# Odd blocks of x read in 128-byte pieces and turned by VectorE; outer-product tables in parts of four heads; a new prologue

## The reference

```python
def _L0_cond_ref(u, length, log_dt, C, log_A_real, A_imag, D):
    u_m = u * mask[:, None, :]
    kernel = _get_kernel(log_dt, C, log_A_real, A_imag, Lq)   # [H, L]: 2 Re sum_n Cs exp(dtA l)
    y = irfft(rfft(u_m, 2L) * rfft(kernel, 2L))[..., :L]
    return (y + u_m * D[:, None]) * mask[:, None, :]
def _L0_ffn_ref(x, route_w, A, Bw):                # E=8 experts, rank R=16
    logits = einsum('bsd,ed->bse', x, route_w)
    route_weight = one_hot(argmax(logits)) * max(logits)
    h = einsum('bsd,erd->bser', x, A)
    return einsum('bser,eor->bso', route_weight[..., None] * h, Bw)
x = x + _L0_ffn_ref(_L0_cond_ref(x, ...), ...)
```

## Time and profile before

| | us |
|---|---|
| median of 3 runs | 623.53 |
| profiled execution | 623.93 |
| its span | 622.1 |
| TensorE busy | 591.5 (95%) |
| VectorE busy | 542.5 (87%) |
| ScalarE busy | 379.3 (61%) |
| GpSimd busy | 372.9 (60%) |

### The profile page before, as it was taken

The page is one execution under the profiler, slowest core; times in us unless marked ns, Lnnn a source line. Parts: engine busy times, 40 slices in busy tenths (PEclk is TensorE's granted clock), DMA queues, the critical chain, the costliest instruction groups (busy, mean ns, idle before and its releaser), DMA issues.

```text
span 622.1 us, 13886 instructions
## 1 busy us (share of the span) xinstructions
PE 591.5 (95%) x3681; PEld 530.9 (85%) x3681; DVE 542.5 (87%) x1436; ACT 379.3 (61%) x1164; POOL 372.9 (60%) x474
## 2 busy tenths in 40 slices
PE   3379999999999999999999999999999999999995
PEld 2268998999899889988998998899899989988984
DVE  7778889988988898899889888988998898889874
ACT  3676656766676666567666766665676667666520
POOL 4465566557656755675576567556755765676520
PEclk9989999999999999999999999999999999999998
DMA  6023534453454345435534543454345345434521
GB/s 137 17 56 108 152 110 128 147 150 96 142 149 132 113 139 153 112 126 146 152 96 139 151 133 110 141 152 114 125 146 152 98 136 151 139 105 140 154 78 67
DMA packets 37074, 77.68 MB, mean 125 GB/s; under 512 B 11836, under 2 KB 20350, under 8 KB 36998
## 3 DMA queue, kind: packets, MB, share of 16 engines
q1 hardware_dynamic: 27846, 43.76, 29.5%
q10 hardware_dynamic: 9152, 33.03, 13.0%
HBM read 43.16 MB, written 33.62 MB: 123 GB/s over the span
## 4 chain that ended last, share of the span: by engine, by line
PE 92%; DVE 4%; issue 2%; POOL 1%; ACT 0%; DMA 0%; POOLq 0%
PE psYo L987 19%; PE psZ L1009 19%; PE psO L987 15%; PE psYe L987 12%; PE psS L987 11%; PE psO L1036 5%; PE psXe L1000 4%; PE psXo L1000 4%; PE psZ L1078 1%; PE psS L1047 1%; DMA logs<-in_L_cond_log_dt_dram 0%; DVE ex L693 0%; POOL Grev L436 0%; POOL wave L426 0%; DVE fraction L803 0%
## 5 line engine op out<-in xcount | busy, mean ns | idle before, releaser
L468 POOL TENSOR_TENSOR Slo<-Sf,Shi 128x384 fp32r<-128x384 f32 x64 | 64.9, 1015 | 210.1 <-ACT Shi L590 210.1
L852 DVE SCALAR_TENSOR_TENSOR brought<-Sf,tab,psS 64x128 f32<-64x128 f32 x256 | 89.0, 348 | 47.3 <-ACT Sf L585 40.9
L1009 PE MATMUL psZ<-Wt,Y 128*128 128x136 f32 x1024 | 129.6, 280 | 0.0
L1009 PEld LDWEIGHTS psZ<-Wt,Y 128*128 128x128 f32 x1024 | 127.8, 191 | 0.1
L531 ACT ACTIVATE Ghi<-Grev 128x256 fp32r<-128x256 f32 x64 | 26.8, 418 | 94.2 <-POOL Grev L436 94.2
L884 DVE TENSOR_TENSOR ost<-psO,xt 128x512 f32<-128x512 f32 x128 | 82.0, 676 | 2.2 <-PE psO L987 2.2
L461 POOL TENSOR_TENSOR Xlo<-xeven,Xhi 128x512 fp32r<-128x512 f32 x64 | 82.8, 1293 | 0.0
L568 ACT ACTIVATE Xhi<-psXe 128x512 fp32r<-128x512 f32 x64 | 38.2, 597 | 38.3 <-PE psXe L1000 38.3
L789 DVE TENSOR_SCALAR whole<-turns_t 128x256 f32<-128x256 f32 x64 | 57.8, 903 | 4.1 <-ACT turns_t L519 4.1
L585 ACT ACTIVATE Sf<-psS 128x128 f32<-128x128 f32 x64 | 17.7, 277 | 66.4 <-PE psS L987 66.4
L987 PE MATMUL psYo<-Xhi,Thi 128*128 128x512 f32 x128 | 55.6, 434 | 0.0
(11 more groups left out here) (194 smaller groups left out, 1670.8 us busy)
## 6 DMA issues: line engine op xcount, KB each, us to landing
xt<-in_x_dram SPq DMA_DIRECT2D x64, 512.0 KB, 4.1
out_dram<-ost ACTq DMA_DIRECT2D x63, 512.0 KB, 4.8
Traw<-kdram SPq DMA_DIRECT2D x64, 128.0 KB, 2.9
kdram<-krow SPq DMA_DIRECT2D x64, 1.0 KB
A_nat<-in_L_ffn_A_dram SPq DMA_DIRECT2D x1, 512.0 KB, 4.9
B_nat<-in_L_ffn_Bw_dram SPq DMA_DIRECT2D x8, 64.0 KB, 3.6
out_dram<-ost SPq DMA_DIRECT2D x2, 256.0 KB, 2.0
lens_i<-in_itok_B_dram SPq DMA_DIRECT2D x1, 64.0 KB, 3.6
```

What stands on the lines that cost most here:

```text
L468: pool.tensor_tensor(Slo[h.s2][:, :], Sf[h.s2][:, :], Shi[h.s2][:, :].bitcast(F32), ALU.subtract).then_inc(slo_done, 1)
L852: dve.scalar_tensor_tensor(brought[to, :], Sf[h.s2][fr, old], tab2[fr, BR, h.n:h.n + 1], psS[to, new], ALU.mult, ALU.add).then_inc(brought ...
L1009: last = pe.matmul(psZ[:, 0:NW], Y[:, j, c, :], Wt[:, 2 * c + j, :], start=(j == 0 and c == 0), stop=(j == 1 and c == NE - 1), skip_group_ ...
```

## The change

The change has three parts.

First, the odd blocks of x no longer come from TensorE. SyncE reads them from DRAM a second time, in 16 DMAs per head (`load_blocks`): each brings 32 partitions x 4 pieces of 32 floats, so that 32 x 32 squares of the block lie where VectorE's transpose (which turns squares of 32 x 32) leaves the whole block turned. VectorE turns all 4 odd blocks in one instruction, `xodd<-xblk` of 128 x 512. ScalarE copies the result to `Xhi`, and the odd low part goes from VectorE to GpSimd. Four TensorE transposes per head go.

Second, the 256-column tables are outer products of two 16-column tables, coarse and fine. The angles, sines and weights of these are made for four heads at a time (a `Part`), and per head GpSimd makes one 512-column product and one 256-column sum.

Third, the prologue is another one: head 0's step is written out in it, SyncE loads the blocks of heads 0 to 2 in it (those of head 0 ahead of `B_nat`), and TensorE waits for `B_nat` before the first `inputs`.

```diff
+            def load_blocks(h):
+
+                need(sp, xodd_done, h.n - 1)
+                for g in range(G4):
+                    for c in range(NE):
+                        sp.dma_start(xblk[h.s2][g * G32:(g + 1) * G32, c, :, :],
+                                     bass.AP(x.tensor, h.n * L + c * Q + P + g * G32,
+                                             [[H * L, G32], [G32 * H * L, G4], [1, G32]])
+                                     ).then_inc(blk_in[h.s2], 16)
@@ SyncE, step
                 if head(2).there:
+                    load_blocks(head(2))
                     load_x(head(2))
                     write_kernel(head(2))
                     skew_kernel(head(2))
@@ SyncE, prologue
+            load_blocks(Head(0))
             with nc.allow_non_contiguous_dma(reason="expert rows of 16"):
...
             load_x(Head(1))
+            load_blocks(Head(1))
+            load_x(Head(2))
             sp.wait_ge(pad_done, 32)
-            for n in range(2):
+            for n in range(3):
                 write_kernel(Head(n))
                 skew_kernel(Head(n))
+                if n == 1:
+                    load_blocks(Head(2))
@@ VectorE
+            def turn_blocks(h):
+
+                need(dve, blk_in[h.s2], (h.half + 1) * 16 * G4 * NE)
+                need(dve, xlo_odd, h.n)
+                dve.transpose(xodd[:, :], xblk[h.s2][:, :, :, :].rearrange("p c g i -> p (c g i)")
+                              ).then_inc(xodd_done, 1)
...
             def step(head):
+                if head(1).there:
+                    turn_blocks(head(1))
                 if head(0).there:
                     carry(head(0))
...
+                if part_at(head(6)):
+                    whole_turns(part_at(head(6)))
@@ GpSimd
+            def x_lo_odd(h):
+
+                need(pool, xhi_odd, h.n + 1)
+                need(pool, y_mm, (h.n - 1) * 2)
+                pool.tensor_tensor(Xlo[h.s2][:, 1, :], xodd[:, :], Xhi[h.s2][:, 1, :].bitcast(F32),
+                                   ALU.subtract).then_inc(xlo_odd, 1)
...
+                pool.tensor_tensor(
+                    both[:, :, :, :],
+                    coarse[:, :, h.n, :].rearrange("p t (a b) -> p t a b", b=1).to_broadcast(wide),
+                    fine[:, :, h.n, :].rearrange("p t (a b) -> p t a b", a=1).to_broadcast(wide),
+                    ALU.mult).then_inc(both_done, 1)
...
+                pool.tensor_tensor(Grev[h.s2][:, :], both[:, 0, :, :].rearrange("p a b -> p (a b)"),
+                                   both[:, 1, :, :].rearrange("p a b -> p (a b)"), ALU.add).then_inc(grev_done, 1)
@@ TensorE, step
                 if head(0).there:
                     bring(head(0))
+                if head(1).there:
+                    turn_x(head(1))
+                if head(2).there:
+                    inputs(head(2))
                 if head(-1).there:
-                    project(head(-1), 0)
-                    project(head(-1), 1)
...
                 if head(2).there:
                     turn_k(head(2))
-                if is_head(head(0), H):
+                if head(-1).there:
                     turn_wh(head(-1))
@@ TensorE, prologue
+            pe.wait_ge(xeven_done, 1)
+            turn_tables(pack2, psX[0], 5)
             pe.wait_ge(in_B, 16 * E)
+            pe.wait_ge(tab_done, 1)
...
+            inputs(first[0])
+            turn_k(first[0])
+            bring(first[0])
+            turn_x(first[1])
```

More of the change, by code:

```diff
@@ L262, in __init__, with part_at @@
                 self.there = 0 <= n < H
+        class Part:
+            def __init__(self, k, start, stop):
+                self.k = k
+                self.start = start
+                self.n = stop - start
+                self.heads = slice(start, stop)
+        EDGES = list(range(0, H + 1, FIRST))
+        parts = [Part(k, EDGES[k], EDGES[k + 1]) for k in range(len(EDGES) - 1)]
+        def part_at(h):
+            for part in parts[2:]:
+                if part.start == h.n:
+                    return part
+            return None
         def is_head(h, *numbers):
@@ L281, in run_steps @@
         def run_steps(step):
-            for i in range(H + 1):
+            for i in range(1, H + 1):
                 step(lambda d, i=i: Head(i + d))
@@ L409, in _, with angle_steps @@
             pool.wait_ge(tab_done, 1)
[L410 to L420, removed]
+            def angle_steps(part):
+                need(pool, turns_done, part.k * 4)
+                need(pool, frac2_done, part.k * 2)
+                for t, table in ((step_h, VH), (step_t, V), (step_l, VL)):
+                    pool.tensor_tensor(t[:, 0:part.n, :],
+                                       tab1[:, table, part.heads].rearrange("p (h a) -> p h a", a=1)
+                                       .to_broadcast([P, part.n, G16]),
+                                       grid16[:, :].rearrange("p (a g) -> p a g", a=1)
+                                       .to_broadcast([P, part.n, G16]), ALU.mult).then_inc(steps_done, 1)
@@ L422, in g_table @@
             def g_table(h):
-                need(pool, wave_done, h.n + 1)
+                need(pool, mirrored, 4 * sum(part.start <= h.n for part in parts))
                 need(pool, grev_done, h.n)
+                wide = [P, 2, G16, G16]
                 pool.tensor_tensor(
[L427 to L430, removed]
@@ L475, in step @@
                     x_lo(head(1))
-                if head(3).there:
+                if head(3).there and is_head(head(0), 1):
                     g_table(head(3))
@@ new lines, in mirror @@
+            def mirror(part):
+                need(act, weighed, part.k * 3 + 3)
+                top, low = slice(0, N), slice(N, P)
+                for table, to, half, fr, scale in ((coarse, low, 1, top, 1.0), (coarse, top, 1, low, -1.0),
+                                                   (fine, low, 0, top, 1.0), (fine, top, 1, low, 1.0)):
+                    act.activation(table[to, half, part.heads, :], table[fr, half if table is fine else 0, part.heads, :],
+                                   ACT.Copy, scale=scale).then_inc(mirrored, 1)
@@ L1123, in turn_tables @@
                 last.then_inc(tabs_turned, 1)
[L1125 to L1128 removed]
+            first = [Head(n) for n in range(3)]
+            pe.wait_ge(consts, 9)
+            turn_x(first[0])
             pe.wait_ge(pack1_done, 1)
@@ L1153, in _ @@
                     last.then_inc(b_turned, 1)
+            inputs(first[0])
+            turn_k(first[0])
+            bring(first[0])
+            turn_x(first[1])
             inputs(first[1])
             turn_k(first[1])
-            pe.wait_ge(w_done, 3)
+            within(first[0], 0)
+            within(first[0], 1)
+            inputs(first[2])
+            from_states(first[0])
+            turn_k(first[2])
             run_steps(step)
```

422 lines of the change are left out of this document (229 added, 193 removed).

## The result

The changed kernel takes 837.65 us (median of 4 runs, 834.46 to 843.76), the kernel before, measured beside it, 623.68 us (622.24 to 623.88). The ratio is 1.345, 95% interval 1.337 to 1.353: slower by a third. The forecast was 799 us, with a range of 670 to 960.

What follows compares the result with a forecast made beforehand. SyncE's serial queue was taken as the bound: third skewed read at 46.5 us, 61 turns of 12.0, then 18.9 to the end, span 797.4, so 799 us. Range 670 to 960, the forecast's own 745 to 855.

Steps and rivals of the forecast that it cites:

- The bound: Whole loop: SyncE's serial queue, 12.0 us a head, sets the period instead of TensorE; TensorE busy 70 to 75%.
- Step (a): SyncE's 16 block issues a head: 0.47 us each from start to start, 7.5 us together; 0.37 and 0.63 kept.
- Step (b): SyncE's queue: the row's write lands behind x, 4.1 us from x's issue; its wait grows from 0.88 to almost 4.
- The period: One turn of SyncE's loop: 16 issues, 4.1 us until x and write land, 0.36 for the skewed read; 12.0 us.
- The prologue: Before the loop: third row comes from TensorE at about 46 us, third skewed read issued at about 46.5.
- The end: Behind the last skewed read, issued at 778.5 us: its landing, T's parts, last products and the rest, 18.9 us.
- What TensorE waits for: TensorE in the loop: it waits, through T's parts, for the skewed read, and is busy 70 to 75%.
- A sum: Forecast's own range: one issue, start to start (c), from 0.42 to 0.54 us gives 745 to 855 us, chance 42%.
- Neither decides: VectorE and ScalarE in the loop: VectorE at most 8.4 us a head, under TensorE's 8.55; ScalarE has room.
- Rival 4: On top of rival 3, GpSimd's odd low part holds VectorE's `Sf`: 0.4 us a head, 620 us; fast forms together 9%.
- rival 3: SyncE's write not held by x; fast form: TensorE bounds at 8.55 us, 595 us; 9% with rival 4's fast form.
- Rival 5: TensorE's clock: idling puts every second step at the 1.2 GHz level, mean step 15.2 us, 994 us; chance 3%.

Runs made afterwards that it cites:

- e3: Changed kernel with the block loads of heads 2 to 63 left out, so VectorE turns old pieces; 680.76 us, ratio 1.093 to the kernel before.
- e5: Changed kernel with the row's write and the skewed read moved from SyncE's to ScalarE's queue for heads 3 to 63; 689.66 us, ratio 1.108.
- e4: Changed kernel with the same 16 block issues a head, but from head 2 on 32 pieces each in place of 128; 821.68 us, ratio 1.320.
- e9: Changed kernel with only two VectorE operand changes: `brought` in PSUM, and the gate taking the logits from PSUM; 845.68 us, ratio 1.357.
- e1: Changed kernel with the load of x issued ahead of the 16 block issues instead of behind them; 756.91 us, ratio 1.215.
- e8: e3 with `brought` moved to PSUM and the gate taking the logits from PSUM; 612.20 us, ratio 0.983 to the kernel before.
- e6: e5 with `brought` moved to PSUM and the gate taking the logits from PSUM; 633.06 us, ratio 1.015 to the kernel before.

## Why the prediction was right, and where it was not

**The bound.** Right. Of its signs, TensorE's busy share came out at 76% (70 to 75 named) and the wait for the row's landing at 2.94 us a head (3 or more named). SyncE's loop sets the end; e3 and e5 take 157 and 148 us off by emptying it, e4 and e5 rule out the pieces' transfer, and e9 shows that nothing of VectorE's counts beside it.

**Step (a), the price of an issue.** Right for most: the median is 0.432 us, 0.475 from start to start, against 0.47 taken from two single loads. The reserve that early issues are dearer (0.63) was wrong: head 0's pieces took 7.45 us instead of the 10.1 reckoned. What was missed is a tail. 85 of the 1024 issues take over 0.5 us, up to 2.04, so that groups of 16 took from 7.5 to 9.35 us, 8.15 in the mean of the loop, against the 7.5 forecast for each. This is the term that made the forecast too short.

**Step (b), the row's write behind x.** Right. From x's issue to the skewed read 423.08 - 419.02 = 4.06 us in the turn shown, 3.67 in the one before (410.99 - 407.32), against 4.1 forecast; over the loop it is 3.9 in the mean. x and the row's write land together, as forecast: the chain has the write landing at 407.85 + 3.07 = 410.92, and TensorE, which waits for x, starts at 411.08. e1 put x elsewhere and 1.8 of 2.9 us of wait went.

**The period.** From the third skewed read (45.07) to the last (807.02) lie 61 turns: 762.0 / 61 = 12.5 us against 12.0. That is 30 of the 35 us by which the span is longer than forecast (832.7 against 797.4).

```profile
35.95 7.66 SPq L347 DMA_DIRECT2D xblk<-in_x_dram  x16
...
45.07 0.34 SPq L364 DMA_DIRECT2D Traw<-kdram  x1
...
807.02 0.34 SPq L364 DMA_DIRECT2D Traw<-kdram  x1
```

**The prologue.** The third skewed read was issued at 45.07, forecast 46.5, but not for the forecast's reason. That had the third row come from TensorE at about 46, as the last thing. It was there at 40.25:

```profile
39.98 0.27 ACT L660 ACTIVATE krow<-psZ 2x128 f32<-2x128 f32 x1 [0.57 <-PE psZ L1164]
```

What held its write until 43.71 was the queue, which issued head 2's pieces until 35.95 + 7.66 = 43.61. So the row was nearly 6 us earlier than forecast, and the queue, forecast free at 43.9, and the landing of the write set the time instead; that this number came so close is partly luck. Head 1's pieces were done at 26.8 instead of 30.4, but the second row's write went out only at 33.65 and its read at 35.56 (36.4 forecast), so most of that did not show.

**The end.** The chain goes through the last load of x:

```profile
803.20 4.30 DMA xt<-in_x_dram
```

From there to the end of the span it is 29.5 us. The forecast's terms give 797.4 - 774.4 = 23.0 from the same point. Behind x stand the last two heads' transposes, products and additions; the forecast followed the row and not x. That adds 6.5 us. With the 30 of the turns, less 1.4 for the earlier start, these are the 35.

**What TensorE waits for.** Wrong. One sign named for the forecast was that TensorE waits, through T's parts, for the skewed read. It waits for x (157.8 us), and for `Thi` only 3.3 us in all. x lands with the row's write and is needed first, by the even transposes; `within`, which needs T, comes after the 16 matmuls of `project`. The period is SyncE's either way, but the end of the kernel is not, as said above.

**A sum.** The forecast's own range is worked out wrongly at its upper end: with c = 0.54 the terms give 61 x (16 x 0.54 + 4.46) + 66.8 = 866 us, not 855. The result lies inside either.

**VectorE.** The transpose's 0.7 us was right (0.708), and the odd `Xhi` on ScalarE is no bound. "Neither decides" was right only as long as SyncE does. Rival 4 named the mechanism, GpSimd holding `Sf`: up to 1.29 us of hold, of which 0.9 would be slack, so 0.4 us a head. Measured in e3 the hold is 0.86 for `Sf` ((100.2 - 45.0) / 64), plus 0.66 for `gate`, which it had not named, and taking both away gave 68.6 / 64 = 1.07 us a head (e3 to e8). So the fast form of rival 3 could not have come true: without the loop's new issues on SyncE the kernel stands at 681, not at 595 or 620. The 9% given to a faster kernel were too many.

**The clock.** Rival 5 came in small. Two stretches, in the form of the earlier trace rows:

```profile
413.00:426.00 13.00, 9.59 (x52) 8.51 (x52) 9.38 (x22) 6.11 (x21) 7.10 (x8) 0.91 0.48 122
424.00:426.00 2.00, 2.00 (x11) 2.00 (x10) 1.38 (x4) 1.64 (x6) 0.18 (x1) 0.50 0.40 93
```

From 424 to 426 us the granted clock was 0.50 of full, the 1.2 GHz level, after TensorE had waited 3.41 us for x (up to 423.26); the 16 matmuls of `project` took 3.17 us there and 2.02 a head earlier, at full clock. The mean of the whole execution was 0.91. If only these two levels occur, that is about 18% of the time at the lower one (an estimate from the mean), where rival 5 had half of all steps there. How much of the 12.5 us a head it cost was not measured by itself; SyncE's queue, which pauses for nearly nothing but the row's landing, leaves little room for it.

## What to carry to other kernels

Before work is cut into many small DMAs, multiply their number by the time of one issue in a row of issues (here 0.475 us, with 128 pieces and hardly less with 32) and compare it with the period: the queue engine is an engine like the others, and a long wait in it before the change is the room it has. Within one queue, don't put a small write that something waits for directly behind a large load (e1), or give it another queue (e5). And when work moves to GpSimd or changes its place there, look up which VectorE instructions will run beside it with both inputs in SBUF or as a `tensor_scalar`: an input in PSUM frees them.

## What the runs showed of the hardware

- **A tiny VectorE instruction that starts behind one of GpSimd's can last as long as that one.** `gate`, 128 x 8, took 0.98 us beside a 1.01 us `Slo` in e3. It is a `tensor_scalar` with one tensor input in SBUF; `Sf` has two. The same work with one of the inputs in PSUM (e6) took 0.22 us. The stream transpose, which also reads SBUF, was never held: 697 to 714 ns over 64, of which 23 ran beside a GpSimd instruction. The Trainium skill (SBUF — State Buffer, Who interferes with whom) gives both rules: two SBUF inputs contend with GpSimd's reads, and `tensor_scalar` can enter a mode that contends with GpSimd, where whichever was issued first has the shared ports for its whole instruction and the other is blocked. The rows agree with both.
- **A quarter of a microsecond in the order of start decides.** The kernel before had the same `Sf` and the same `gate`, at 352 and 302 ns. `gate` ran beside `Slo` there too, but started 0.2 to 0.3 us ahead of it, and took 0.29; in the one head where `Slo` was first it took 0.96. `Sf` had no GpSimd instruction beside it in 127 of 128 cases. In the changed kernel `Slo` or another of GpSimd's instructions is mostly ahead of `gate`, and the change gives GpSimd the odd low part, which now falls beside `Sf`.

```profile
301.43 0.29 DVE L833 TENSOR_SCALAR gate<-rank,best,top 128x8 f32<-128x8 f32 x1
301.68 1.02 POOL L468 TENSOR_TENSOR Slo<-Sf,Shi 128x384 fp32r<-128x384 f32 x1 [3.25 <-ACT Shi L590]
```

- **Single issues can take over four times the median.** 0.43 us is the median, 2.04 the longest, and with a quarter of the pieces it is 2.07: the length of the long ones does not come from the size either. What causes them is open.
- **A small write issued behind a 512 KB load in the same queue is late with it**: the skewed read, which waits only for the write's landing, was issued 3.1 and 3.5 us behind the write in the two turns shown, against 1.2 before.
